# The second product of the step three back moved ahead of the projection, in PE's order of both token stages

## The reference

```
x = x + conv0(ln_c(x))                      # gated convolution, its last step is w_out
t = to_tokens(x); t = t + ffn0(ln_t(t))     # per pixel, over the 48 channels
x = x + conv1(ln_c(x))                      # wavelet convolution and fusion, its last step is op_w
t = to_tokens(x); t = t + ffn1(ln_t(t))
ffn(t): h = relu(q(t) @ q(W1) + b1); y = q(h) @ q(W2) + b2      # q: to 5 exponent, 2 mantissa bits; sums to 10
```

## Time and profile before

| | |
|---|---|
| median of 3 runs | 2622.57 us (2621.44 to 2628.5) |
| the profiled execution | 2624.89 us, its span 2623.1 us |
| granted clock of PE, mean | 0.938 of 2.4 GHz |
| busy: PE, PE weight loads | 2272.7 us (87%), 1247.5 us (48%) |
| busy: DVE, ACT, POOL | 1523.5 us (58%), 1123.3 us (43%), 450.0 us (17%) |
| DMA | 458.55 MB, mean 175 GB/s |

### The profile page before, as it was taken

How to read it: one execution, slowest core, us unless ns; L and a number is a source line. 1 busy time by engine, 2 the same in 40 slices (tenths; PEclk the granted TensorE clock), 3 DMA queues, 4 the chain that set the end, 5 groups by cost and what they waited for, 6 DMA issues and landing times. The chain is left out here.

```text
span 2623.1 us, 62156 instructions
## 1 busy us (share of the span) xinstructions
PE 2272.7 (87%) x21290; PEld 1247.5 (48%) x21290; DVE 1523.5 (58%) x2653; ACT 1123.3 (43%) x2338; POOL 450.0 (17%) x707
## 2 busy tenths in 40 slices
PE   6679778898996999999699999999976998688886
PEld 3344436667773333333266666666641232233332
DVE  3345401111113777777488888888842455577776
ACT  4346421111112888888532222222211111577776
POOL 7510015100100000000054444444410000000000
PEclk9789869999997999999899999999987999899999
DMA  6999989788874777877576666666628999333332
GB/s 154 260 254 270 253 284 303 230 263 262 285 245 91 142 142 146 152 142 145 100 155 144 142 142 142 142 143 143 144 86 162 240 267 237 87 102 106 105 102 78
DMA packets 533239, 458.55 MB, mean 175 GB/s; under 512 B 316476, under 2 KB 445444, under 8 KB 529778
## 3 DMA queue, kind: packets, MB, share of 16 engines
q1 hardware_dynamic: 462882, 425.87, 63.4%
q0 software_dynamic: 5744, 23.34, 3.7%
q10 hardware_dynamic: 64512, 7.88, 2.3%
HBM read 272.33 MB, written 186.40 MB: 175 GB/s over the span
## 5 line engine op out<-in xcount | busy, mean ns | idle before, releaser
L604 PE MATMUL gate_ps<-gate_data,gate_wt 64*64 64x289 f32 x6144 | 397.1, 416 | 39.2 <-issue 27.2
L604 PEld LDWEIGHTS gate_ps<-gate_data,gate_wt 64*64 64x64 f32 x6144 | 303.1, 136 | 134.3 <-issue 59.8
L662 DVE TENSOR_TENSOR gate_out<-gate_gelu,gate_ps 128x578 f32<-128x578 f32 x96 | 72.2, 756 | 399.3 <-PE gate_ps L604 343.7
L949 ACT CAST mix_h<-mix_bank 96x512 f16<-96x512 f32 x512 | 267.6, 593 | 7.1 <-PE mix_bank L900 3.2
L639 ACT ACTIVATE gate_gelu<-gate_ps 128x578 f32<-128x578 f32 x96 | 62.7, 653 | 367.8 <-PE gate_ps L604 331.2
L2036 PE MATMUL fus_bank<-fus_xt,fus_taps 76*32 76x512 f32 x1344 | 159.6, 626 | 28.4 <-DMA fus_shift<-gate_shift 23.5
L1031 DVE TENSOR_SCALAR mix_hb<-mix_h,mix_b1q 96x1024 f16<-96x1024 f16 x256 | 122.7, 479 | 93.6 <-ACT mix_h L949 93.6
L900 PE MATMUL mix_bank<-mix_xq,mix_w1q 112*96 112x512 fp8e5 x512 | 143.5, 382 | 29.1 <-ACT mix_h L949 23.0
L1039 DVE CAST mix_hq<-mix_hb 96x2048 fp8e5<-96x2048 f16 x128 | 156.5, 1223 | 19.5 <-DVE mix_hb L1031 16.9
L292 DVE COPY exp_out<-exp_y 128x384 f32<-128x384 f32 x192 | 102.1, 567 | 103.5 <-PE exp_y L255 52.1
L912 PE MATMUL mix_x_bank<-mix_hq,mix_w2q 96*112 96x512 fp8e5 x512 | 136.1, 388 | 29.9 <-DVE mix_hq L1039 27.7
(11 more groups left out here) (226 smaller groups left out, 4050.6 us busy)
## 6 DMA issues: line engine op xcount, KB each, us to landing
y<-exp_out SPq DMA_DIRECT2D x64, 816.0 KB, 12.2
gate_data<-y SPq DMA_DIRECT2D x24, 2176.0 KB, 17.6
g<-gate_out SPq DMA_DIRECT2D x48, 578.0 KB, 4.9
mix_sc<-g SPq DMA_DIRECT2D x31, 816.0 KB
gate_wt<-wm SPq DMA_DIRECT2D x96, 256.0 KB, 8.5
wav_strips<-xp SPq DMA_DIRECT2D x96, 204.0 KB, 3.8
wav_halves<-xp SPq DMA_DIRECT2D x48, 340.0 KB
init<-wav_init SPq DMA_DIRECT2D x48, 268.0 KB, 2.4
```

The costliest lines, as they stand in the source:

```text
L604: mm = pe.matmul(banks(a, v)[64 * g:64 * (g + 1), r], wt[q][64 * r:64 * (r + 1), 2 * a + g, n, :], src, start=n == 0, stop=n == 3)
L949: act.copy(h16[at.pair][:, m, h, :], bank[(2 * m + h) % len(bank)][0:HID, :]).then_inc(h16_ready, 1)
```

## The change

The second product (show) of step k-3 is issued ahead of the projection of step k, in PE's list of both stages. All else stays.

```
-                pieces = [(0, project), (3, show), (2, hide(0)), (2, hide(1)), (1, variance("in")), (0, centre_in)]
+                pieces = [(3, show), (0, project), (2, hide(0)), (2, hide(1)), (1, variance("in")), (0, centre_in)]
                 if norm_dst is not None:
-                    pieces = [(0, project), (3, show), (2, hide(0)), (4, centre_out), (2, hide(1)), (1, variance("in")), (5, variance("out")), (0, centre_in)]
+                    pieces = [(3, show), (0, project), (2, hide(0)), (4, centre_out), (2, hide(1)), (1, variance("in")), (5, variance("out")), (0, centre_in)]
                 staged(pe, 2 * N, SLOTS, pieces, LEAD)
```

## The result

The changed kernel took 2682.23 us in the median of 4 runs (2680.34 to 2691.8), the kernel before 2625.53 (2621.44 to 2630.09, 4 runs). The ratio is 1.0223, with an interval of 1.0191 to 1.0254. The medians differ by 56.7 us, against a forecast of 54, and 2682 lies in the range of 2653 to 2694. In time the interval reaches from 50 to 67 us.

A forecast was written before the change was run, and what follows sets the result against it. Prediction: second stage bound by a loop of second product, casts, bias and quantisation, first by nearly full PE; 37 + 17 = 54 us over the 2622.6 median gives 2677 us, range 2653 to 2694 (forecast's own bounds 2665 to 2692).

The forecast's parts named there:

- Slower, by a wait that is not shortened and a projection that comes to stand behind it: Both stages: second product still waits for DVE, projection queues behind it; 54 us slower in sum, chance of slower 0.95.
- Second stage, 0.60 a step, 37 us: Second stage: 0.26 of the projection's 0.86 us absorbed, 0.60 not; step 6.24 against 5.64, over 61 steps.
- The second path, through DVE: Second stage: DVE waits for the projection's end before the residual add, 1.65 us of waiting; step 6.22 us.
- First stage, 0.28 a step, 17 us: First stage: goes from held by PE to the second stage's loop; step 7.22 against 6.93, lower bound 9 us.
- early in the first stage: Rival, first stage: second product starts early, saving 0.11 a step, 7 us; with second stage losing 37, 2653 us; chance 0.04.
- The slack in the second stage: Rival, second stage: ACT's idle 1.4 us a step takes the later hidden product at no cost; 2616 us; chance 0.03.
- The clock: Rival: granted clock falls, half of the second stage at 1.2 GHz, 72 us more; about 2749 us; chance 0.05.
- the second stage would have lost nothing: Rival "nothing shows", second stage: projection's two passes hold PE only 0.26 us by the page's figure; 2622 us; chance 0.02.

The follow-up runs named there:

- e3_half_hidden_first: Kernel before, second stage alone reordered on PE: second product, first half of the hidden product, projection, second half; ratio to before 1.0214.
- e8b_hidden_first: Kernel before, with hidden product (first stage: its first half) and its casts ahead of the second product, projection still first; ratio to before 1.0251.
- e5b_double_before: Kernel before, old order kept, with the matmul of the second stage's projection issued twice; ratio to before 1.0122.

## Why the prediction was right

- **Slower, by a wait that is not shortened and a projection that comes to stand behind it.** Shown. The second product started when the quantisation was done, as before; the projection got in behind it; PE's idle time before the second product grew from 0.30 to 1.33 or 1.51 us, and the doubling showed that this idle time has no room.
- **Second stage, 0.60 a step, 37 us.** Measured 38.2 us, 0.63 over the same 61 steps. Term by term in the timeline above: second product to next group 0.88 (predicted 0.88), projection's hold 0.86 (0.86), hidden product to first cast 0.42 (0.42), cast to second bias 2.07 (2.08), bias to next second product 2.00 (2.00). The second path, through DVE, was also as predicted: the wait for the projection is 1.49 in this step and 1.69 in the next. The chain of waits passes over one path and the other in turn:

```profile
2481.84 0.23 PE mix_bank L900
2482.57 1.57 ACT mix_h L949 x3
...
2487.20 0.87 PE mix_x_bank L864 x2
...
2488.98 0.35 DVE mix_yb L1045
...
2490.06 0.88 DVE mix_hb L1031 x2
```

  After the second product of 2479.93 it goes by the hidden product and ACT's casts, after that of 2486.16 by the projection and DVE's adds. So the steps are 6.23 and 6.29 us in turn, 0.62 more than before on average. The two paths are so near each other that shortening one alone should gain next to nothing; no run does that by itself. e3_half_hidden_first shortened the first and lengthened the second by 0.43, and the step followed the second.
- **First stage, 0.28 a step, 17 us.** The mechanism was right, with its order of releasers, and the size too small: 24.2 us. The steady step is 7.33 (911.70 to 919.03) where the sum gave 7.22. The term that was mis-sized is the time from the second product to what follows it. I took 0.90 from the hidden product that stood there; with the projection there it is 0.97 (911.70 to 912.67), and the first cast followed its product by 0.45 where I had 0.42. The half to the next second product was 3.68 (predicted 3.67). These two terms make 0.10 of the 0.11. A further 0.01 is in the prediction's own sum, which took 0.28 where 7.22 against 6.93 is 0.29. So the mis-sized terms are worth 7 us.
- **Sum.** 62.4 us in the stages against 54. The median of the changed kernel came 5 us over the forecast. The medians alone, with their interval of 50 to 67 us, can't tell 54 from 62; that they differ by less than the stages do is chance as far as these runs tell.
- **The rivals.** None came about. The second product was not early in the first stage: it waited for the logarithm each time. The slack in the second stage did not take the projection. The clock was 1.00 through both steady parts, with more idle time on PE than before. The Trainium skill ("TensorE: Matmul & The Clock Gate", "A second HAM failure mode: psum-queue depth-cycling") tells of frequent small idle times of PE that make the clock go back and forth. With waits of 1.33 and 1.51 us in each step the steady part of the changed kernel does not bear that out. In e8b_hidden_first, with waits of up to 2.2 us, the clock did go back and forth, so this rival was a live one for orders near to this. A pass of the projection holds PE 0.43 us and each matmul of the second product 0.22, behind the change as before it. The Trainium skill's figure of some 131 ns for a matmul of 512 columns (same page, "Back-to-back issue gap") is not borne out: by that figure the second stage would have lost nothing where it lost 38 us.
- **What the prediction expected of the profile** came as written but for two numbers. It had some 452 us for the quantisations of the first stage, and they took 459.6. It put PE's idle time before the second product at 1.7 us in the second stage; it is 1.33 to 1.51, since part of PE's idle time went ahead of the variance, which waits for the residual add.

## What to carry to other kernels

In a pipeline of in-order engines, find the loop that sets the step before moving anything. A piece that its engine does while it would wait for another one anyway is free where it is. Once it stands behind that wait it costs what no other wait absorbs: here 0.6 of the projection's 0.86 us in the second stage, and 0.80 of a further 0.86 when it was doubled. Idle time in front of an instruction is room only for what may be issued ahead of it. And when a loop is cut, look at once for what is next in every queue, the DMA issuer's included, and at the granted clock: here a load behind a store, with the falls of the clock that came with it, cost more than the cut had gained, until the store was moved.

## What the runs showed of the hardware that was not expected

- A product whose weight load does not lie ahead of it costs 0.09 us more here. In the second stage the projection (112 by 112) starts 0.88 behind the second product, its weight load at 2480.60 lies 0.21 ahead of its matmul, and the projection holds PE 0.86. The averaging product of the same step has the same shape, but its load waits for DVE and starts with its matmul (2482.68 for both); it holds PE 0.95 (2482.68 to 2483.63). The doubled projection of e5b_double_before, behind a wait, shows the same 0.09.

```profile
2480.60 0.39 PEld L864 LDWEIGHTS mix_x_bank<-mix_sc,mix_proj 112*112 112x112 f32 x2
...
2482.68 0.27 PEld L887 LDWEIGHTS mix_x_bank<-mix_sq_in,mix_average 112*112 112x112 f32 x2 [0.45 <-DVE mix_x L1017]
```

- In the first stage the projection (96 rows and 48 columns of weights, L858) starts 0.97 us behind the second product, where the hidden product started 0.90 behind it. Its first weight load starts with its first matmul (912.67 for both), though no other engine is named for it. It was so before the change too, behind the centring (911.97 for both, 0.95 after the centring's start). What keeps this load from lying ahead, no run here tells.

```profile
912.67 0.17 PEld L858 LDWEIGHTS mix_x_bank<-mix_sc,mix_proj 96*48 96x48 f32 x4 [0.39 <-issue]
```

- In e8b_hidden_first the granted clock fell to 0.50 and came back within the steady part of the second stage. After a wait of PE of 1.84 us that ended at 2459.99 it was 0.50 from 2461.5 to 2464.5, and the second product held PE 1.71 us there (2462.09 to 2463.80) and not 0.86; after the wait of 1.83 us that ended at 2448.17 it stayed at 1.00. So the length of a single wait does not say, in this trace, whether the clock falls.
